# Attention stage of a decoder layer: the value products of two units placed next to each other, and nine places for the exponentials

## The reference, cut to what matters

```python
q = (x @ Wq.T + bq).reshape(B, N, HEADS, HEAD_DIM).transpose(0, 2, 1, 3)
k = (context @ Wk.T + bk).reshape(...)      # likewise, and v
attn = softmax(einsum('bhnd,bhmd->bhnm', q, k) * scale, axis=-1)
out = einsum('bhnm,bhmd->bhnd', attn, v)
x = layernorm(x + out @ Wo.T + bo)
```

## Time and profile before

| | us |
|---|---|
| median of 3 runs | 1916.67 (1914.59 to 1917.23) |
| the profiled execution's own time | 1913.56 |
| its span in the profile | 1911.8 |
| attention stage, first to last transposed score | 865.0 to 1620.6 |
| PE busy in the span | 1806.3 (94%) |
| DVE busy | 1415.7 (74%) |
| ACT busy | 1255.3 (66%) |
| value products (line 2197), busy | 139.6, 1024 instructions |
| exponentials (line 1969), busy | 299.9, 512 instructions |
| TensorE clock granted, mean | 0.979 |

### The profile page before, as it was taken

The page is one execution under the profiler, slowest core; times in us unless marked ns, Lnnn a source line. Parts: engine busy times, 40 slices in busy tenths (PEclk is TensorE's granted clock), DMA queues, the critical chain, the costliest instruction groups (busy, mean ns, idle before and its releaser), DMA issues. The chain is left out here.

```text
span 1911.8 us, 38932 instructions
## 1 busy us (share of the span) xinstructions
PE 1806.3 (94%) x12588; PEld 1285.0 (67%) x12588; DVE 1415.7 (74%) x2902; ACT 1255.3 (66%) x3128; POOL 527.2 (28%) x789
## 2 busy tenths in 40 slices
PE   7899999999999999779999999999999998699988
PEld 5677777778787877555666666666666663588853
DVE  8988888888887879646676767676777776555348
ACT  5646464555555555348888888988989888256514
POOL 1312121212131312341333333333343433100006
PEclk9999999999999999988999999999999999799999
DMA  7122131313131312333344444444443435712266
GB/s 237 53 52 101 47 106 46 107 41 112 36 117 35 118 36 95 133 106 105 101 123 123 123 123 123 123 113 134 112 134 112 132 81 169 228 46 67 67 209 253
DMA packets 126700, 209.25 MB, mean 109 GB/s; under 512 B 26416, under 2 KB 49456, under 8 KB 126256
## 3 DMA queue, kind: packets, MB, share of 16 engines
q1 hardware_dynamic: 112176, 179.21, 30.6%
q0 software_dynamic: 14336, 27.55, 5.6%
HBM read 125.66 MB, written 30.15 MB: 81 GB/s over the span
## 5 line engine op out<-in xcount | busy, mean ns | idle before, releaser
L2039 DVE TENSOR_REDUCE a_mx<-a_shared 128x1 f32<-128x512 f32 x512 | 327.5, 678 | 51.3 <-PE a_shared L2169 50.6
L1976 ACT ACTIVATE a_shared<-a_shared,a_mx 128x512 f32<-128x512 f32 x512 | 341.6, 669 | 23.0 <-DVE a_mx L2039 22.5
L1969 ACT ACTIVATE a_probs<-a_scores 128x512 f32<-128x512 f32 x512 | 299.9, 600 | 55.5 <-PE a_scores L2186 52.1
L2169 PE MATMUL a_shared<-a_ks,a_qs 96*128 96x512 f32 x512 | 209.0, 429 | 14.9 <-ACT a_shared L1976 9.7
L2186 PE MATMUL a_scores<-a_qs,a_ks 98*128 98x512 f32 x512 | 201.8, 406 | 5.0 <-ACT a_probs L1969 4.9
L2141 PE MATMUL a_shared<-link 128*128 128x512 f32 x768 | 199.0, 395 | 2.0 <-DVE a_qk_lo L2026 2.0
L1083 PE MATMUL m_proj<-m_xt_hi,link 128*128 128x512 f32 x448 | 182.0, 406 | 4.2 <-DVE m_acc L777 3.5
L597 ACT ACTIVATE m_xw<-m_added,m_wdt 128x64 f32<-128x64 f32 x256 | 55.8, 329 | 193.0 <-DVE m_xdt L865 192.9
L1084 PE MATMUL m_proj<-m_xt_lo,link 128*128 128x512 f32 x448 | 176.4, 394 | 0.0
L1085 PE MATMUL m_proj<-m_xt_hi,link 128*128 128x512 f32 x448 | 176.0, 393 | 0.0
L777 DVE SCALAR_TENSOR_TENSOR m_acc<-m_proj,m_cw,m_acc 128x511 f32<-128x511 f32 (+2 forms) x216 | 159.3, 747 | 16.8 <-ACT m_acc L536 11.7
(11 more groups left out here) (307 smaller groups left out, 3939.9 us busy)
## 6 DMA issues: line engine op xcount, KB each, us to landing
m_dec<-step_decay SPq DMA_DIRECT2D x64, 256.0 KB, 4.1
a_qs<-link SPq DMA_DIRECT2D x256, 64.0 KB, 2.0
m_ce<-run_decay SPq DMA_DIRECT2D x128, 112.0 KB, 3.1
a_ks<-a_k_hi POOLq DMA_DIRECT2D x192, 64.0 KB, 2.5
e_x<-x SPq DMA_DIRECT2D x11, 1024.0 KB, 5.6
m_xt_in<-x_t_in SPq DMA_DIRECT2D x8, 1024.0 KB, 9.2
m_x_tok<-x_in SPq DMA_DIRECT2D x8, 1024.0 KB, 5.5
x<-m_x_tok SPq DMA_DIRECT2D x32, 256.0 KB, 2.8
```

What stands on the lines that cost most here:

```text
L1969: act.activation(probs[:, n % 2, h, :], scores[t.score_bank(n, h)][:, :], ACT.Exp, scale=-1.0).then_inc(exp_ready, 1)
L1976: act.activation(scored[:, :], scored[:, :], ACT.Exp, scale=-1.0, bias=mx[:, i % 2, h, j:j + 1], accum_out=den[:, i, h, j:j + 1]).then_inc ...
L2039: dve.tensor_reduce(mx[:, i % 2, h, j:j + 1], bank(what)[:, :], AX.X, ALU.min).then_inc(mx_ready, 1)
L2169: pe.matmul(bank(what)[:, :], qs[0:STACK, t.slot(i), h, j * P:(j + 1) * P], ks[0:STACK, t.slot(i), h, :], start=True, stop=True).then_inc( ...
```

## The change

The value products of units n − 2 and n − 1 now follow each other, in every even unit n, behind the first head's transposed score (and behind the half projection that stands there in units 6, 10, 12 and 14). In odd units there is none. `norm` moves with them: it stands behind the second of the pair in u = 0. All other steps keep their order and places; so `neg` and `inv` stay at the ends of their units.

Since the exponential of the first head of an even unit is now written before the products of unit n − 2 have read `probs`, there is a ninth place: that exponential uses place 0 and place 8 in turn (`probs_place`). The wait of ACT on `av` stands ahead of the second head's exponential of an even unit, once for two units. To make room, `inv_t` and `neg` become two partition ranges of one tile. The rename of `d` to `ahead` in the last loop keeps the variable `d` for its new use.

```diff
+def probs_place(n, h):
+    place = AG * (n % 2) + h
+    return place if place or n // 2 % 2 == 0 else 2 * AG
...
     for n in range(UNITS):
         gr, u = divmod(n, TT)
+        group, d = (gr - 1, 0) if n >= TT else (KT - 1, -1)
...
                 if HALF_AT[n][half] == h:
                     large(n, half)
-        group, d = (gr - 1, 0) if n >= TT else (KT - 1, -1)
-        put("av", *((gr, u - 1, 0, 0) if u else (group, TT - 1, 0, d)))
+            if h == 0 and u % 2 == 0:
+                pair, turn = (gr, 0) if u else (group, d)
+                for j in range(2):
+                    put("av", pair, (u or TT) - 2 + j, 0, turn)
+                if u == 0:
+                    put("norm", group, 0, 0, d)
         totals(LAGS[3])
-        if u == 0:
-            put("norm", group, 0, 0, d)
...
-        neg = sb("neg", [2 * AG * TT, P], F32R)
+        turned = sb("turned", [3 * AG * TT, P])
+        neg, inv_t = turned[0:2 * AG * TT, :], turned[2 * AG * TT:3 * AG * TT, :]
...
-        probs = sb("probs", [P, 2, AG, SEQ])
+        probs = sb("probs", [P, 2 * AG + 1, SEQ])
...
-                    if h == 0 and (n >= 2 or not t.first()):
-                        act.wait_ge(av_done, t.at(UNITS, n - 1))
-                    act.activation(probs[:, n % 2, h, :], scores[t.score_bank(n, h)][:, :], ACT.Exp,
+                    if h == 1 and n % 2 == 0 and (n or not t.first()):
+                        act.wait_ge(av_done, t.at(UNITS, n))
+                    act.activation(probs[:, probs_place(n, h), :], scores[t.score_bank(n, h)][:, :], ACT.Exp,
...
-                                        probs[:, n % 2, hh, :], start=(j == 0), stop=(j == TT - 1))
+                                        probs[:, probs_place(n, hh), :], start=(j == 0), stop=(j == TT - 1))
```

More of the change, by code:

```diff
@@ L1550, in attention_order @@
             put("spread", gr, 0, 0, 0)
-        for i, d in STACKED.get(n, ()):
-            put("stack", i, 0, 0, d)
+        for i, ahead in STACKED.get(n, ()):
+            put("stack", i, 0, 0, ahead)
         if u == 1:
@@ L1694, in attention_stage @@
         next_x = nc.alloc_sbuf_tensor_at("a_next_x", [P, TT, SEQ], F32, offset=NEXT_X)
-        probs = sb("probs", [P, 2, AG, SEQ])
+        probs = sb("probs", [P, 2 * AG + 1, SEQ])
         den = sb("den", [P, KT, AG, TT])
         inv = sb("inv", [P, KT, AG, TT])
-        inv_t = sb("inv_t", [AG * TT, P])
         o_hi = sb("o_hi", [P, KT, SEQ], F32R)
@@ L1876, in step @@
                         sp.dma_start(qs[STACK + r:STACK + r + 1, t.slot(i)].bitcast(F32),
-                                     neg[r * AG * TT:(r + 1) * AG * TT, :].bitcast(F32)).then_inc(neg_in[i % 2], 16)
+                                     neg[r * AG * TT:(r + 1) * AG * TT, :]).then_inc(neg_in[i % 2], 16)
             over_attention(sp, n_seq, step, steps)
```

## The result

The changed kernel takes 1986.58 us (median of 4 runs, 1983.74 to 1987.68) against 1915.63 for the kernel before (4 runs, 1911.54 to 1917.23): 1.0371 times as long, 95% interval 1.0355 to 1.0386. It is 71 us slower; the forecast was 32 slower, with an upper end of 1970. The direction was right and the size was not.

What follows compares the result with a forecast made beforehand. PE was taken to set the pace, with ACT having little to spare. A steady pass gains 4.3 us; seven passes +30, the last +2: +32 on 1913.56, so 1945.6, about 1948 as median; 8-in-10 range 1927 to 1970.

Steps and rivals of the forecast that it cites:

- A pair then costs ... 2.04: On PE, two value units together cost 2.04 us instead of 2.40, saving 0.36 a pair, 2.9 a pass.
- A lonely `inv` isn't in the trace; its bounds are 0 and 0.41, and I take 0.41: On PE, `inv` alone among wide products costs 0.41 us, taken from a lonely `neg` in unit 2.
- the seven places: Four lonely `inv` at 0.41 us and three `neg` (units 6, 10, 14) at 0.30: 2.5 us a pass on PE.
- so the waits add: 4.4 us: PE waits for late ACT exponentials at transposed scores and pairs, in seven stretches, 4.4 us a pass.
- The wait spreads to the banks: Rival, chance 0.19: with ACT late, `p1` and projections wait for banks, 0.7 us in two places a pass: 1959 us.
- The forecast's sum of a steady pass: PE's list −0.4, waits for ACT +4.4, some 0.05 us at each of seven starts: +4.3 us a pass.
- one in unit 8: In the kernel before, a score product of unit 8 stands 0.52 us until ACT has emptied a bank.
- the bank rival: Waits spreading to banks, 1959 us, chance 0.19; its sign: idle time stands ahead of `p1`.
- nothing that could run is held: On DVE, the earlier-queued `norm` delays only maxima of products that PE issues after the pair; no cost.
- The last pass: +2 forecast: The last pass has no projections to hide under; half of PE's 5.4 us idle time is taken: +2 us.

Runs made afterwards that it cites:

- norm_back: The changed kernel with `norm` put back at the end of unit u = 0, the pair left in place: 1987.51 us, 1.0349 times the kernel before.
- nosum: Kernel before and changed kernel, each with the sums' exponentials cut to one column and `p1`'s bank free at DVE's maximum: 1901.16 and 1948.22 us.
- nosum_after: The changed kernel with the sums' exponentials cut to one column and `p1`'s bank free at DVE's maximum: 1948.22 us, 1.0157 times the kernel before.
- quick_bank: The changed kernel without the sums, DVE's low part of q and k projections reading ACT's copy instead of the bank: 1939.68 us, 1.0113 times the kernel before.

## Why the prediction was wrong in size

1. *"A pair then costs ... 2.04"*: right; 1.86 us to the next product where 1.85 was forecast.
2. *"A lonely `inv` isn't in the trace; its bounds are 0 and 0.41, and I take 0.41"*, and the same for `neg`: wrong. A lonely `neg` costs 0.12 in the place shown; behind a lonely `inv` a wait follows within two products, so its price can't be read by itself. The row from which 0.41 came holds a wait besides the transpose, and it is one for a bank. Timeline of the kernel before, between its first and last row:

```profile
1363.37 0.27 DVE L2055 COPY a_inv_t<-a_shared 16x128 f32<-16x128 f32 x1
1363.42 0.27 PE L2174 MATMUL a_shared<-a_ident,a_mx_split 128*32 128x128 f32 x1
1363.69 0.53 PEld L2141 LDWEIGHTS a_shared<-link 128*128 128x128 f32 x3 [0.40 <-DVE a_inv_t L2055]
```

The projection starts 0.27 us behind `neg`, 0.05 behind the end of DVE's copy of `inv`'s bank; in the changed kernel it starts 0.03 behind `neg` (1415.17 to 1415.20). That is 0.24 of the 0.29 too much, and it was a bank's way back in the trace before any run. With 0.12 for 0.41 in the seven places PE's list is 2.4 us shorter a pass, not 0.4 (2.6 is what the pass and the counted pauses leave). This error was in the kernel's favour.
3. *"so the waits add: 4.4 us"*: the size is near to what ACT's work turned out to be worth, the place is not, so the nearness is luck. Without the sums the gap between the two kernels shrinks from 7.9 to 4.4 us a pass, so some 3.5 hang on ACT's work; halving them takes away 1.9. But ACT is late with the sums, which hold the banks of `p1`; at the transposed scores and the pairs, where I put it, PE loses 2.1 us a pass in all.
4. *"The wait spreads to the banks ... one more 0.7 us in two places of a pass"*: this is the step that failed. The forecast's sum of a steady pass (−0.4 + 4.4, and 0.3 for the starts) has no term for banks at all, and the rival has 1.4 us; measured are 12.0 us of pauses where there were 1.5, more than 8 of the 12.0 at `p1` and the projections, where banks are claimed. I took the bank waits as what a late ACT causes, found one in unit 8 and priced two. They don't need a late ACT. The products of the values were the work without a bank between a unit's last half projection and the next claims; with that cover gone a bank's ordinary way back (for q and k ACT's copy of 0.73 us, DVE's 0.75 us and 0.06 to the claim; for v DVE's 0.69 us and 0.05) is longer than the work ahead of its next turn, in many places of a pass. I priced how late ACT's results come and never how late banks come free, though the list gives both in the same manner: claim, last reader, release, next claim. The sign that the prediction set down for the bank rival is what the trace shows: the idle time stands ahead of `p1`.
5. *"nothing that could run is held"* by `norm`: right in steady passes, wrong in the last, where it holds DVE for 4.91 us.
6. The last pass: +2 forecast (half of its 5.4 us of idle time, which is rather 2.7), +14.6 measured. `norm` explains 5.2. The clock has a part too: it falls during the stand of 5.38 us that ends at 1666.24, and is at its lower level for some 20 us of this pass, in the kernel before for some 7 (means 0.88 and 0.96). Work in these 13 to 14 us more would have taken half at full clock, so I estimate 7 us at most; norm_back's mean is 0.92, so part of this is in `norm`'s 5.2. A window of the changed kernel:

```profile
1664.50:1674.60 10.10, 8.01 (x18) 3.96 (x22) 7.73 (x14) 9.20 (x25) 0.56 (x1) 0.50 0.01 2
```

The forecast had no term for the clock, neither here nor at the turn of the loop. In the other direction some 8 us of the profiled execution come back behind the last score (291.2 us from there to the end before, 283.0 after), and the start of the stage is 2.8 us later. Neither need be the change's doing: over the profiles of all runs the end takes 282.2 to 291.2 us and the start 863.4 to 869.2.

The sum, the sixth pass: −2.6 for the list and +10.5 for the pauses (12.0 − 1.5) is +7.9. Of the pauses some 3.5 go with the sums and 7 stay without them, by nosum, of which some 5 are named as waits for banks; the two are not independent, since a sum too holds a bank, so the split is rough. Seven passes make +61 (between 7.0 and 12.7 each, with some 6 us around the turn of the loop), the last +14.6, the start +2.8, the end −8.2: +70, which is the difference of the two profiled executions (1983.74 − 1913.56).

## What to carry to other kernels

Work that claims no buffer is cover for the buffers around it. Before you move such a block, write down for each claim in its old neighbourhood when that buffer's last reader ends, and shift the claims by what you take away; a claim that stands 0.1 us behind its release costs nothing now and nearly the whole shift afterwards. A duration that is read as a distance between two starts may contain a wait: look at what stands between the two, and for the same distance in a second place, before it enters a sum. And a total inside the range set for one theory doesn't choose between two: nosum_after's did not, the place of its pauses did.

## What the runs showed of the hardware

In quick_bank DVE's low part has both inputs in the buffers instead of one in a bank. By line, with the duration of one in ns (min/median/max), for the two halves of these instructions:

```profile
L2037 DVE SCALAR_TENSOR_TENSOR a_qk_lo<-a_k_hi,bcol x32: 750/752/3526, 826.8 to 1556.2; 128x512 fp32r<-128x512 f32 x32
L2037 DVE SCALAR_TENSOR_TENSOR a_qk_lo<-link,bcol x32: 750/751/753, 830.6 to 1568.8; 128x512 fp32r<-128x512 f32 x32
```

Seven are long (1.76 to 3.53 us), each of them lies beside an addition of POOL, and none that starts beside one stays at 0.75. The timeline of the sixth pass:

```profile
1448.71 4.65 POOL L1918 TENSOR_TENSOR a_x_tok<-a_x_tok,a_brow 128x2048 f32<-128x2048 f32 x1
1450.72 3.19 DVE L2037 SCALAR_TENSOR_TENSOR a_qk_lo<-a_k_hi,bcol 128x512 fp32r<-128x512 f32 x1 [1.54 <-ACT a_k_hi L1972]
```

DVE took 3.19 us instead of 0.75: 2.64 until POOL's end at 1453.36 and 0.55 more. The Trainium skill, SBUF — State Buffer, section Who interferes with whom, says that a DVE instruction with two inputs in SBUF contends with a GpSimd instruction that reads SBUF, through a read interface that the two share. These rows agree. In nosum_after, where one of the two inputs is in a bank, all seven of these instructions that run beside the same addition take 0.75 us.

Of the clock: in the changed kernel PE stood 2.26 us, did two products and stood 3.46 us; within the second stand, at 1289.0, the granted clock fell to its lower level, 0.50, for 6.8 us; the sixteen value instructions took 3.57 us there and 1.86 at 1.00.

The price of a lonely transpose of 32 columns among wide products is 0.12 us in the row shown; that of sixteen narrow value products in a row is 1.86 where two times eight would be 2.00.
